# Two tiles per scalar-engine statistics pass, and 18 tiles of statistics instead of 24 on the vector engine

## What is computed

```python
g = group_norm(x)                      # 32 groups of 4 channels, statistics over the whole image
u = mean(g, axis=channel)              # per pixel
s = sqrt(var(g, axis=channel, ddof=1))
n = (g - u) / (s + 1e-6)
y = einsum('bchw,oc->bohw', n, W) + b
out = g + g * y                        # x + conv_ref(x), on the group-normed x
```

## Time and profile before

| | |
|---|---|
| time, median of 3 runs | 1894.35 us (1892.35 to 1896.38) |
| profiled execution, its own time | 1890.62 us |
| its span (first to last instruction) | 1888.8 us |
| granted TensorE clock | 0.996 of full |
| PE / DVE / ACT / POOL busy | 90% / 91% / 77% / 77% of the span |
| moved by DMA | 667.33 MB, 353 GB/s over the span |

### The profile page before, as it was taken

The page is one execution under the profiler, slowest core; times in us unless marked ns, Lnnn a source line. Parts: engine busy times, 40 slices in busy tenths (PEclk is TensorE's granted clock), DMA queues, the critical chain, the costliest instruction groups (busy, mean ns, idle before and its releaser), DMA issues.

```text
span 1888.8 us, 67606 instructions
## 1 busy us (share of the span) xinstructions
PE 1699.3 (90%) x28706; PEld 920.7 (49%) x28706; DVE 1727.5 (91%) x2120; ACT 1446.4 (77%) x2498; POOL 1458.4 (77%) x1684
## 2 busy tenths in 40 slices
PE   0079998999989999999999999899999999899998
PEld 0045554555545555455555555455545555455553
DVE  5669999999999999999999999999999999988887
ACT  5589886888868986798869889688877898644442
POOL 0068787888878887888878787787877888788885
PEclk9989999999999999999999999999999999999999
DMA  9979999999999999999999999899999999854775
GB/s 375 407 285 375 375 373 327 390 394 391 364 339 406 375 396 342 344 407 382 383 323 393 400 386 381 314 402 386 397 349 340 416 373 397 290 205 189 276 264 221
DMA packets 183036, 667.33 MB, mean 353 GB/s; under 512 B 20560, under 2 KB 20944, under 8 KB 182736
## 3 DMA queue, kind: packets, MB, share of 16 engines
q1 hardware_dynamic: 109008, 394.54, 56.9%
q10 hardware_dynamic: 73728, 268.47, 35.4%
HBM read 394.49 MB, written 268.44 MB: 351 GB/s over the span
## 4 chain that ended last, share of the span: by engine, by line
PE 68%; DVE 18%; issue 6%; DMA 3%; SPq 2%; ACT 2%; POOL 1%; POOLq 0%; ACTq 0%; DVEq 0%
PE proj_ps L731 40%; PE sums_ps L719 15%; PE factor_ps L705 12%; DVE scaled L629 5%; DVE bn L673 4%; DVE bn L674 4%; DMA tiles<-x 3%; SPq L410 2%; DVE tiles L642 1%; DMA out<-tiles 1%; DVE gn L583 1%; ACT unused L511 1%; ACT squares L526 0%; DVE gn L587 0%; POOL tiles L454 0%
## 5 line engine op out<-in xcount | busy, mean ns | idle before, releaser
L731 PE MATMUL proj_ps<-scaled,w_t 128*32 128x512 f32 x8192 | 985.9, 599 | 0.1
L454 POOL TENSOR_SCALAR tiles<-tiles,columns_sb 128x1024 f32<-128x1024 f32 x512 | 576.9, 1127 | 257.4 <-DVE tiles L642 254.4
L642 DVE SCALAR_TENSOR_TENSOR tiles<-proj_ps,columns_sb,tiles 128x1024 f32<-128x1024 f32 x512 | 643.3, 1257 | 69.1 <-PE proj_ps L731 67.5
L511 ACT ACTIVATE unused<-tiles,bn 128x1024 uint8<-128x1024 f32 x560 | 635.2, 1134 | 0.0
L443 POOL TENSOR_SCALAR tiles<-tiles,columns_sb 128x1024 f32<-128x1024 f32 x512 | 620.4, 1212 | 12.9 <-DMA tiles<-x 11.7
L629 DVE TENSOR_TENSOR scaled<-tiles,factor_ps 128x1024 f32<-128x1024 f32 x512 | 619.0, 1209 | 7.2 <-PE factor_ps L705 2.1
L526 ACT ACTIVATE squares<-tiles 128x1024 f32<-128x1024 f32 x512 | 537.8, 1050 | 81.3 <-POOL tiles L443 37.0
L719 PEld LDWEIGHTS sums_ps<-tiles,const_sb 128*32 128x32 f32 x8192 | 245.8, 111 | 316.3 <-issue 265.2
L731 PEld LDWEIGHTS proj_ps<-scaled,w_t 128*32 128x32 f32 x8192 | 213.6, 109 | 360.8 <-issue 306.8
L705 PE MATMUL factor_ps<-pieces,pick_sb 128*128 128x128 bf16 x4096 | 318.1, 221 | 77.2 <-DVE scaled L629 72.5
L719 PE MATMUL sums_ps<-tiles,const_sb 128*32 128x128 f32 x8192 | 320.6, 275 | 11.7 <-ACT squares L526 11.7
(11 more groups left out here) (56 smaller groups left out, 782.3 us busy)
## 6 DMA issues: line engine op xcount, KB each, us to landing
tiles<-x SPq DMA_DIRECT2D x752, 512.0 KB, 8.6
out<-tiles ACTq DMA_DIRECT2D x512, 512.0 KB, 7.1
const_sb<-const SPq DMA_DIRECT2D x1, 85.5 KB, 1.9
scaled<-w SPq DMA_DIRECT2D x1, 64.0 KB, 2.0
scaled<-ident SPq DMA_DIRECT2D x1, 64.0 KB, 1.8
pick_sb<-pick SPq DMA_DIRECT2D x1, 8.0 KB, 2.0
columns_sb<-bias SPq DMA_DIRECT2D x1, 0.5 KB, 2.1
```

The costliest lines, as they stand in the source:

```text
L454: nc.gpsimd.tensor_scalar(place(s), place(s), 1.0, out_shift[:, 0:1], ALU.mult, ALU.add).then_inc(finished, 1)
L511: nc.scalar.activation(unused[:, which, :], data, (ACT.Identity, ACT.Square)[which], bias=pivot_of(of), scale=-1.0, accum_out=act_sums[:, ...
L642: nc.vector.scalar_tensor_tensor(out=place(s), in0=proj_ps[:, s % 2, :], scalar=gate_shift[:, 0:1], in1=place(s), op0=ALU.add, op1=ALU.mul ...
L731: mm = nc.tensor.matmul(proj_ps[q:q + 32, s % 2, h:h + BANK], w_t[:, q:q + 32], scaled[:, s % 2, h:h + BANK], start=True, stop=True)
```

## The change

Four things are changed together. ACT's tiles are taken in pairs: one pass runs over two tiles (128 x 2048), so a pair needs two passes in all where two tiles needed four. DVE's share in full periods falls from 24 tiles to 18, so ACT's rises from 40 to 46, which is 23 pairs and 46 passes. No pass stands between the two pieces or ahead of `sum_sq` any more (`SUM_SQ_AFTER = 0`, and the call between the pieces is gone): each pass stands at the end of its step. And the planned lead of a statistics load falls from 2 steps to 1, with another numbering of the buffers, so that both tiles of a pair lie at a constant distance.

```diff
-STATS_DVE = 24
+STATS_DVE = 18
...
-STATS_LEAD = 2
+STATS_LEAD = 1
...
-    passes = 2 * (slots - dve)
+    passes = slots - dve
     at = [PIVOT_STEP + 1 + p * (until - PIVOT_STEP - 1) // passes for p in range(passes)]
-    begun += [(at[p] + 0.5, "act", at[p:p + 2]) for p in range(0, passes, 2)]
+    begun += [(at[p] + 0.5, "act", at[p:p + 2]) for p in range(0, passes, 2) for _ in range(2)]
...
+ORDER = [(p + 36) % BUFFERS for p in range(BUFFERS)]
...
-        SUM_SQ_AFTER = 1
+        SUM_SQ_AFTER = 0
...
             def statistics(n, step, of, count):
-                for i, which in todo[:count]:
-                    data = wait_stats_data(act, n, i)
-                    a = of.index[i]
+                for a, which in todo[:count]:
+                    for i in of.pairs[a]:
+                        wait_stats_data(act, n, i)
+                    low, high = sorted(places.buffer["stats", i] for i in of.pairs[a])
...
-                    nc.scalar.activation(unused[:, which, :], data, (ACT.Identity, ACT.Square)[which], bias=pivot_of(of),
+                    nc.scalar.activation(unused[:, :, :], tiles[:, low:high + 1:high - low, :],
+                                         (ACT.Identity, ACT.Square)[which], bias=pivot_of(of),
                                          scale=-1.0, accum_out=act_sums[:, which, a:a + 1]).then_inc(act_done, 1)
...
                         nc.scalar.activation(piece[:, :], factor[:, :], ACT.Identity, scale=at["rows_bc"]).then_inc(piece_a_done, 1)
-                        statistics(b + 1, step, of, 1)
                         act.wait_ge(rest_done, done)
```

More of the change, by code:

```diff
@@ L120, in __init__ @@
         for k in range(len(kept)):
-            self.put(("stats", drops + k), k)
+            self.put(("stats", drops + k), ORDER[k])
         for s in streamed:
@@ L154, in free @@
     def free(self, kind, i):
-        found = [p for p in range(BUFFERS) if min(self.room(p, (kind, i))) >= 0]
+        found = [p for p in ORDER if min(self.room(p, (kind, i))) >= 0]
         assert found, (kind, i, self.span[kind, i])
@@ L181, in __init__, with at, passes_at @@
         self.bn_slots, self.act_slots = self.engine.count("dve"), self.engine.count("act")
-    def at(self, step, engine):
-        return [(i, p) for i, steps in enumerate(self.steps) if self.engine[i] == engine
-                for p, t in enumerate(steps) if t == step]
+        act = [i for i, engine in enumerate(self.engine) if engine == "act"]
+        self.pairs = [tuple(act[a:a + 2]) for a in range(0, self.act_slots, 2)]
+    def at(self, step):
+        return [i for i, steps in enumerate(self.steps) if self.engine[i] == "dve" and step in steps]
+    def passes_at(self, step):
+        return [(a, which) for a, (i, _) in enumerate(self.pairs)
+                for which, t in enumerate(self.steps[i]) if t == step]
 def norm_gate_kernel(nc, x, w, bias, const, pick, ident, out):
@@ L210, in act_before @@
             return 0
-        return n * (2 * plan.act_slots) + 2 * (first_plan.act_slots - plan.act_slots)
+        return n * plan.act_slots + (first_plan.act_slots - plan.act_slots)
     with ExitStack() as ctx:
@@ L234, in norm_gate_kernel @@
         bn = sb("bn", [P, 2 * plan.bn_slots, 6])
-        act_sums = sb("act_sums", [P, 2, max(plan.act_slots, first_plan.act_slots)])
+        act_sums = sb("act_sums", [P, 2, max(len(plan.pairs), len(first_plan.pairs))])
         gn = sb("gn", [P, 16])
@@ L384, in wait_item_done @@
                 else:
-                    sp.wait_ge(act_done, act_before(n) + 2 * (of.index[i] + 1))
+                    sp.wait_ge(act_done, act_before(n) + 2 * (of.index[i] // 2 + 1))
             def wait_buffer_free(tenant, b):
@@ L507, in statistics @@
                     done = 2 * a + which
-                    if n > 0 or done >= 2:
-                        act.wait_ge(act_done, act_before(n) + (done - 1))
-                    nc.scalar.activation(unused[:, which, :], data, (ACT.Identity, ACT.Square)[which], bias=pivot_of(of),
+                    if n > 0 or done >= 1:
+                        act.wait_ge(act_done, act_before(n) + done)
+                    nc.scalar.activation(unused[:, :, :], tiles[:, low:high + 1:high - low, :],
+                                         (ACT.Identity, ACT.Square)[which], bias=pivot_of(of),
                                          scale=-1.0, accum_out=act_sums[:, which, a:a + 1]).then_inc(act_done, 1)
@@ L520, in period @@
                     if nxt:
-                        todo.extend(of.at(step, "act"))
+                        todo.extend(of.passes_at(step))
                     if own:
@@ L583, in gn_scalars @@
                     then(nc.vector.bn_aggr(cell(0, 2), bn_of(of)[:, 0:2 * of.bn_slots, :].rearrange("p a b -> p (a b)")))
-                    dve.wait_ge(act_done, act_before(n) + 2 * of.act_slots)
-                    then(nc.vector.reduce_sum(cell(2, 2), act_sums[:, :, 0:of.act_slots], AXIS_X))
+                    dve.wait_ge(act_done, act_before(n) + of.act_slots)
+                    then(nc.vector.reduce_sum(cell(2, 2), act_sums[:, :, 0:len(of.pairs)], AXIS_X))
                     then(nc.vector.tensor_scalar(cell(2, 2), cell(2, 2), 1.0 / total, None, ALU.mult))
@@ L669, in period @@
                     if nxt:
-                        for i, _ in of.at(step, "dve"):
+                        for i in of.at(step):
                             data = wait_stats_data(dve, b + 1, i)
```

## The result

The changed kernel takes **1933.87 us** (median of 5 runs, 1933.39 to 1934.48), the kernel before 1892.35 us in 5 runs. The ratio is 1.0214 (95% interval 1.02 to 1.0228): slower by 41.5 us. 1938 was forecast, in a range of 1896 to 1958. The profiled execution took 1934.48 us.

What follows compares the result with a forecast made beforehand. PE, without slack, waits for DVE's multiply. Per full period 11.86 us lost less 4.92 and 0.33 gained is 6.61; with the first period 45.5, less 2 for loads, +43.5 us: 1938 us, range 1896 to 1958.

Steps and rivals of the forecast that it cites:

- the price of a doubled step: A phase 3 step where DVE has two tiles of statistics delays PE 0.82 us; 9 per full period become 3.
- The pass behind `sum_sq`: Phase 0 passes on ACT hold up the root, so PE's phase 2 spread: 0.69 us per on-time set, 11 passes a period.
- The price of a pass: A 2048-wide pass holds ACT 1.98 us, against 1.13 for one of 1024.
- The sum by sets: Losses per full period, sets named by first step, late meaning ACT reaches `sum_sq` late after phase 2 and 3 passes: 11.86 us.
- The aggregation: DVE aggregates 216 values instead of 288 while PE waits: 0.33 us gained per period.
- Loads: POOL's late streamed tiles near a period's end get more time: 2 us off in all, bounds nothing and 8.
- Fill and last period stay: Pipeline fill and last period unchanged, since batch 0's last loads are still DVE's: no cost.
- The signs: New profile: some 20 PE spread waits a period, not 11; DVE waits 1.5 us for approx; DVE busy falls 57 us.
- The faster one: Rival: what stands behind `sum_sq` is covered, so only DVE's relief shows: 1858 us, chance 0.12.
- Not added up: Rival: ACT is always back on time for `sum_sq`, 5.5 us lost against 5.25 gained: about 1896 us, chance 0.08.
- Transfers are no bound: Judges the rival that 376 GB/s is a ceiling, so relieving engines gains nothing: 1894 us a floor, chance 0.03.
- Pairs waiting for loads: Rival: ACT waits 3 us once or twice a period for both tiles to land: 1960 to 1980 us, chance 0.07.

Runs made afterwards that it cites:

- the mix: Changed kernel with 15 tiles on DVE, 14 pairs in wide passes, 21 single tiles in narrow ones, nothing behind `sum_sq`: 1854.18 us, ratio 0.979 to the kernel before.

## Why the prediction was right

*What bounds, and the price of a doubled step.* Right: 0.82 us each in every full period, and 33 us for 41 of them when taken away alone. The pass behind `sum_sq` as the cause of the loss was right too: it is seen in the timeline, goes with the passes (1855.31 us), and goes with their place (1891.51 us).

*The price of a pass.* 1989 ns for one of 2048, and 1.99 us to the next instruction, where I had 1.98 from the slope between two rows:

```profile
L522 ACT ACTIVATE unused<-tiles,bn 128x2048 uint8<-128x2048 f32 x322 | 640.4, 1989 | 0.0
...
L594 DVE BATCH_NORM_AGGREGATE gn<-bn 128x2 f32<-128x216 f32 x7 | 7.8, 1119 | 0.0
```

The 1.99 us that the Trainium skill (ScalarE: Activation LUTs, What ACT_TABLE_LOAD costs) gives agrees with the trace, 1989 ns.

*The sum by sets,* for the period from 1011 to 1239 us, from PE's spreads:

| sets | forecast | measured |
|---|---|---|
| on time, pass in phase 0 (8, 12, 28, 44, 48) | 3.45 | 0.93 + 0.70 + 3 x 0.69 = 3.70 |
| late behind a late set (24) | 1.85 | 0.11 + 1.72 = 1.83 |
| late (36, 56) | 3.36 | 1.62 + 1.64 = 3.26 |
| behind a doubled step (4, 20; 40) | 1.72; 1.03 | 0.82 + 0.81; 1.01 |
| late, no pass in phase 0 (16, 32, 52) | 0.45 | 0.11 + 0.09 + 0.11 = 0.31 |
| together | 11.86 | 11.74 |

Set 8 costs 0.24 us more than the 0.69 of its kind. Its phase 1 step has one small DVE copy ahead of the gate (the gate's shift, L650), which I had not counted:

```profile
1042.25 0.95 DVE L671 RECIPROCAL approx<-approx 128x128 f32<-128x128 f32 x1 [1.58 <-ACT approx L543]
1043.12 0.10 DVE L650 COPY columns_sb<-new_scalars 128x1 f32<-128x1 f32 x1
1043.26 1.28 DVE L653 SCALAR_TENSOR_TENSOR tiles<-proj_ps,columns_sb,tiles 128x1024 f32<-128x1024 f32 x1
1044.46 1.21 DVE L640 TENSOR_TENSOR scaled<-tiles,factor_ps 128x1024 f32<-128x1024 f32 x1
```

From the reciprocal's start to the multiply's it takes 2.21 us here and 1.98 (1113.07 to 1115.05) in the set from 28. With DVE relieved alone the same set loses 0.07, which is these 0.24 less the 0.17 of slack.

*The aggregation.* It fell by 1444 - 1119 = 325 ns, as the slope said. In the one full period of before in which step 59 is on time, step 60 is late by 2.06 us, in the change by 1.82 to 1.85, so 0.21 to 0.24 of the 0.33 came through. In the other full periods of before step 59 is late itself, by 0.2 to 1.2, and step 60 by 1.89 to 1.95, so only 0.04 to 0.13 of the term is seen there.

*Loads.* In some periods of before the steps 59 and 61 were late by up to 1.2 and 1.9 us, where POOL waited for loads; in no full period of the change were they. A mean full period took 222.6 us before and 228.4 now: 5.8 us more, where my sum was 6.6 less a little for loads. In the first period and its fill 8.2 us were added instead of 5.9. The wait for batch 0's statistics grew from 87.7 to 89.7 us, a term that I had put at nothing ("Fill and last period stay"):

```profile
PE sums_ps L753 <- DVE gn L605: 89.7, 1, 89.7
```

*Luck.* The six full periods added 35 us where my sum had 39.7, and the first added 8.2 where it had 5.9. The 2 us taken off for loads, a guess within 0 to 8, and these two misses nearly cancel; so the total says less for the method than the table does. The range of the forecast alone, 1918 to 1955, is also not quite its terms: 8 + 10 us each way of 1938 is 1920 to 1956.

*The signs.* PE's spread waits 16 times in a full period, not some 20, and DVE's busy time fell by 67 us in all, not 57. The other signs came as written.

*The rivals.* The faster one was real as a half, 1860.81 us for DVE's relief alone; its condition, that what stands behind `sum_sq` is covered, is not met. "Not added up" fell: the late sets cost 1.62 to 1.83 us. Transfers are no bound at 376 GB/s, since the mix moves 385. Pairs waiting for loads did not happen in the change's full periods, yet decide what the faster versions are worth.

## What to carry to other kernels

When work is put "at the end of the step", list what stands behind it in the same engine's queue and who waits for that; here 0.17 us of slack decided, and passes 0.85 us longer in that place, 11 in a period, cost more than six vector-engine tiles gave. Fit each filler to the wait it fills: narrow ones where the engine waits anyway, wide ones where the next deadline is a step away. And when a stall goes, read who is next: here it was the load, which made a step late only in the shorter periods.

## What I had not expected of the hardware

Load and store together ran at 384 to 386 GB/s over whole periods of 216 to 218 us in the mix (378 in the last full one), with a DMA share of 0.98 to 1.00. The HBM limit of about 358 GB/s per core that the Trainium skill (DMA: Bandwidth & Descriptors, Specifications) gives, as half of a stack's 716, is no ceiling in these runs, whose kernel runs on one core. A schedule drawn up from row durations held within 0.1 us for the single sets of a whole period, apart from set 8 (0.24 off), step 60 and the loads.
